# Running sums of a linear attention from pairs of tokens, in whole 32-bit products

## The reference, cut to what matters

```python
x = L0_attn_x
xn = _layernorm(x, axis=-1)
x = x + _L0_attn_ref(xn, ...) + _L0_ffn_ref(xn, ...)     # experts: top 2 of 8
# in _L0_attn_ref, per batch and head, with q, k after rope and elu + 1:
def step(carry, qkv):
    K_sum, KV = carry
    q_t, k_t, v_t = qkv
    K_sum = K_sum + k_t
    KV = KV + k_t[..., :, None] * v_t[..., None, :]
    num = jnp.einsum('bhd,bhde->bhe', q_t, KV)
    den = jnp.maximum(jnp.einsum('bhd,bhd->bh', q_t, K_sum), EPS)
    return ((K_sum, KV), num / den[..., None])
xn = _layernorm(x, axis=-1)
x = x + _L1_attn_ref(xn, ...) + _L1_ffn_ref(xn, ...)     # ffn reads x_prev, the token before
```

## Time and profile before

| what | value |
|---|---|
| median of three runs | 368.72 us |
| the profiled execution's own time | 367.48 us |
| its span, first to last instruction | 365.7 us |
| PE busy, of the span | 347.7 us (95%) |
| DVE busy | 317.6 us (87%) |
| ACT busy | 276.1 us (75%) |
| POOL busy | 204.3 us (56%) |
| granted TensorE clock, mean | 0.999 of full speed |

### The profile page before, as it was taken

The page is one execution under the profiler, slowest core; times in us unless marked ns, Lnnn a source line. Parts: engine busy times, 40 slices in busy tenths (PEclk is TensorE's granted clock), DMA queues, the critical chain, the costliest instruction groups (busy, mean ns, idle before and its releaser), DMA issues.

```text
span 365.7 us, 9318 instructions
## 1 busy us (share of the span) xinstructions
PE 347.7 (95%) x2534; PEld 299.9 (82%) x2534; DVE 317.6 (87%) x623; ACT 276.1 (75%) x774; POOL 204.3 (56%) x239
## 2 busy tenths in 40 slices
PE   7999988799899999999999899999999899999986
PEld 2788534499799999999999799989989688788875
DVE  3998799559989999999699979998996799998665
ACT  3887967777686877787878767787895987778752
POOL 3899118844234465756665648675857448883110
PEclk9999999999999999999999999999999999999999
DMA  6842848555355555655654554756642102221112
GB/s 182 217 124 74 325 192 234 173 149 134 108 133 137 139 143 146 170 139 150 175 143 135 152 161 129 186 150 152 148 115 70 31 2 57 57 61 29 30 29 59
DMA packets 45521, 47.00 MB, mean 129 GB/s; under 512 B 6928, under 2 KB 33712, under 8 KB 45216
## 3 DMA queue, kind: packets, MB, share of 16 engines
q1 hardware_dynamic: 40288, 36.88, 33.6%
q0 software_dynamic: 4320, 8.86, 11.5%
q10 hardware_dynamic: 864, 0.67, 0.7%
HBM read 32.88 MB, written 13.50 MB: 127 GB/s over the span
## 4 chain that ended last, share of the span: by engine, by line
PE 76%; DVE 14%; issue 3%; ACT 3%; DMA 2%; ACTq 1%; DVEq 0%
PE banks L546 16%; PE banks L534 14%; PE banks L674 6%; PE banks L675 6%; PE banks L330 3%; PE banks L983 3%; PE banks L1010 2%; PE banks L299 2%; PE banks L524 2%; PE banks L1039 2%; PE banks L321 2%; PE banks L1019 2%; PE banks L993 2%; PE banks L1057 2%; DVE cq L686 2%
## 5 line engine op out<-in xcount | busy, mean ns | idle before, releaser
L468 POOL DMA_INDIRECT xg<-xn_rows,slot_tok x71 | 74.8, 1053 | 74.2 <-PE banks L524 61.7
L563 ACT ACTIVATE xT<-banks,b1T 128x128 f32<-128x128 f32 x284 | 81.1, 371 | 15.4 <-PE banks L534 14.7
L546 PE MATMUL banks<-w_sb,xT 128*128 x568 | 79.6, 283 | 0.0
L485 POOL DMA_INDIRECT qk_exp<-expert_rows,ranki x64 | 63.7, 996 | 21.6 <-issue 17.9
L534 PE MATMUL banks<-xgT,w 128*128 128x128 f32 x568 | 75.3, 276 | 0.0
L546 PEld LDWEIGHTS banks<-w_sb,xT 128*128 128x128 f32 x568 | 69.3, 192 | 1.2
L534 PEld LDWEIGHTS banks<-xgT,w 128*128 128x128 f32 x568 | 69.0, 192 | 0.0
L686 DVE TENSOR_TENSOR cq<-banks,phi 128x360 f32<-128x360 f32 (+1 forms) x96 | 47.4, 548 | 19.1 <-PE banks L675 18.9
L652 ACT CAST high<-outer 128x1152 fp32r<-128x1152 f32 x32 | 37.1, 1158 | 21.6 <-DVE outer L641 21.2
L658 DVE TENSOR_TENSOR low<-outer,high 128x1152 fp32r<-128x1152 f32 x32 | 43.3, 1352 | 3.2 <-ACT high L652 3.2
L695 DVE TENSOR_REDUCE sums<-cq 128x144 f32<-128x1152 f32 x32 | 42.9, 1341 | 0.0
(11 more groups left out here) (205 smaller groups left out, 702.7 us busy)
## 6 DMA issues: line engine op xcount, KB each, us to landing
w<-in_L_ffn_W SPq DMA_DIRECT2D x71, 256.0 KB
expert_rows<-ye SPq DMA_DIRECT2D x71, 64.0 KB
expert_rows<-x_sb SPq DMA_DIRECT2D x2, 2048.0 KB, 10.6
x_sb<-in_L_attn_x SPq DMA_DIRECT2D x8, 256.0 KB, 4.3
xn_rows<-xn SPq DMA_DIRECT2D x8, 256.0 KB, 2.3
w_sb<-in_L_ffn_W SPq DMA_DIRECT2D x8, 256.0 KB, 4.5
out<-outer SPq DMA_DIRECT2D x7, 256.0 KB, 2.3
xg<-xn_rows,slot_tok POOLq DMA_INDIRECT x71
```

The source lines that it names most:

```text
L468: pool.indirect_dma_start(out=xg[n][:, :], out_offset=None, in_=xn_dram, in_offset=bass.IndirectOffsetOnAxis(ap=slot_tok[:, j:j + 1], axis ...
L485: pool.indirect_dma_start(out=y_moe[:, i, k, :], out_offset=None, in_=y_dram, in_offset=bass.IndirectOffsetOnAxis(ap=ranki[:, 0, k, i:i + ...
L546: last = nc.tensor.matmul(y, hidT[p][:, c, :], w2_sb[:, ds(e * NC + c, 1), :], start=False, stop=(c == NC - 1))
L563: last = nc.scalar.activation(hidT[p][:, c, :], ps[3 + p][:, c * P:(c + 1) * P], ACT.Gelu_apprx_tanh, bias=b1T[:, ds(e * NC + c, 1)])
```

## The change

A batch's two tiles now hold its even tokens (r = 0) and its odd tokens (r = 1), so row p of both is the pair of tokens 2p and 2p + 1. DVE adds the outer products of the two (`attn_pair`, 128 x 1152, once per batch). PE multiplies this sum, as plain 32-bit data, with the triangle that leaves the own row out (`tri_x`) for the even tokens, and with the one that includes it (`tri_r`) for the odd ones. An even token then lacks its own term; POOL computes it as (q . k) v in five small instructions per batch (`attn_own`), and DVE adds it to the sums (`attn_add_own`). `high`, `low` and their casts and subtractions are gone. DVE now makes phi and both outer products of the next batch in the even tile, and the pair in the odd tile. ACT copies both tiles' keys in one place.

The loads and stores of x, of the normalised x and of the output are written so that the two tiles of a batch are one run of 1 KB per partition. In the second layer, blocks of 128 columns are swapped (`block_of`), and `mix` takes four instructions of half the size.

```diff
+    pair = [sbuf(f"pair{n}", [P, HED])[:, :] for n in range(2)]
+    tri_r = sbuf("tri_r", [P, P])
+    tri_x = sbuf("tri_x", [P, P])
...
-    def attn_high(act, b, r, p):
-        i = b * 2 + r
-        act.wait_ge(outer_ready, i + 1)
-        act.wait_ge(den_ready, i + 1)
-        if from_(b, 2 - r):
-            act.wait_ge(cum_ps, b * 2 - (0 if r else 2))
-        nc.scalar.copy(high[kept(r, p)], outer[r]).then_inc(high_ready, 1)
-    def attn_low(v, b, r, p):
-        v.wait_ge(high_ready, b * 2 + r + 1)
-        n = kept(r, p)
-        nc.vector.tensor_tensor(low[n], outer[r], high[n].bitcast(f32), ALU.subtract).then_inc(low_ready, 1)
+    def attn_pair(v, b, p):
+        v.wait_ge(outer_ready, 2 * b + 2)
+        v.wait_ge(den_ready, 2 * b + 2)
+        if b >= 2:
+            v.wait_ge(cum_ps, 2 * b - 2)
+        nc.vector.tensor_tensor(pair[p], outer[0], outer[1], ALU.add).then_inc(pair_ready, 1)
+    def attn_own(pool, b, p):
+        pool.wait_ge(phi_ready, b + 1)
+        if b >= 2:
+            pool.wait_ge(own_used, b - 1)
+        nc.gpsimd.tensor_tensor(own_qk[:, :], phib[p][:, 0, 0:D], phib[p][:, 0, D:2 * D], ALU.mult).then_inc(own_part, 1)
+        q = own_qk[:, :].rearrange("p (h d) -> p h d", d=DH)
+        n = 4 * b + 1
+        for half in (DH // 2, DH // 4):
+            pool.wait_ge(own_part, n)
+            nc.gpsimd.tensor_tensor(q[:, :, 0:half], q[:, :, 0:half], q[:, :, half:2 * half], ALU.add).then_inc(own_part, 1)
+            n += 1
+        pool.wait_ge(own_part, n)
+        nc.gpsimd.tensor_tensor(own_dot[:, :], q[:, :, 0], q[:, :, 1], ALU.add).then_inc(own_part, 1)
...
+        nc.gpsimd.tensor_tensor(own[p][:, :, :], own_dot[:, :].unsqueeze(2).broadcast_to([P, H, E9]),
+                                qkv3[:, 2 * b, 2 * D:NW].rearrange("p (e h) -> p h e", h=H), ALU.mult).then_inc(own_ready, 1)
+    def attn_add_own(v, b, p):
+        v.wait_ge(own_ready, b + 1)
+        v.wait_ge(sums_ready, 2 * b + 1)
+        nc.vector.tensor_tensor(sums[:, 0, :, :], sums[:, 0, :, :], own[p][:, :, :], ALU.add).then_inc(own_used, 1)
...
-        pe.wait_ge(low_ready, i + 1)
-        parts = [(tri_r, kept(r, p))] + ([(ones_r, kept(0, p))] if r else [])
+        pe.wait_ge(pair_ready, b + 1)
+        w = tri_r if r else tri_x
         for n, (lo, hi) in enumerate(HEADS):
             cols = slice(lo * E9 * DH, hi * E9 * DH)
             o = ps[n][:, 0:(hi - lo) * E9 * DH]
-            for m, (w, at) in enumerate(parts):
-                nc.tensor.matmul(o, w[:, :], high[at][:, cols], start=(m == 0), stop=False)
-                last = nc.tensor.matmul(o, w[:, :], low[at][:, cols], start=False, stop=(m == len(parts) - 1))
+            last = nc.tensor.matmul(o, w[:, :], pair[p][:, cols], start=True, stop=True)
...
+    OWN_AT = [max(SUMS_AT[2 * b] - 3, 0) for b in range(B)]
...
+            for lo, to in ((P + 1, 0), (0, P)):
+                t = mix_t[p][m].rearrange("p (b t) -> p b t", t=T)[:, :, to:to + P]
+                last = nc.vector.scalar_tensor_tensor(out=t, in0=xT2_of(p)[:, :, lo:lo + P], scalar=one_mu[:, m:m + 1],
+                                                      in1=t, op0=ALU.mult, op1=ALU.add)
...
             def odd(i):
-                if i + 2 < NT:
-                    attn_keys(act, i // 2 + 1, i % 2, 1 - i // 2 % 2)
-                    attn_high(act, i // 2 + 1, i % 2, 1 - i // 2 % 2)
+                if i % 2 == 0 and i + 2 < NT:
+                    for r in range(2):
+                        attn_keys(act, i // 2 + 1, r, 1 - i // 2 % 2)
...
             pool.wait_ge(logits_read, len(CHUNKS))
+            nc.gpsimd.memset(qkv3[:, :, 3 * D:NW], 1.0).then_inc(ones_ready, 1)
...
+                if j in OWN_AT:
+                    attn_own(pool, OWN_AT.index(j), OWN_AT.index(j) % 2)
...
+                if r == 0:
+                    if b + 1 < B:
+                        phi(v, b + 1, 1 - p)
+                        for t in range(2):
+                            attn_outer(v, b + 1, t, 1 - p)
+                    attn_sums(v, i, r)
+                else:
+                    if b + 1 < B:
+                        attn_pair(v, b + 1, 1 - p)
+                    attn_add_own(v, b, p)
+                    attn_sums(v, i, r)
```

More of the change, by code:

```diff
@@ L60, in constant_table @@
     put("rows_in_front", P * row)
-    put("token_no", P * np.arange(NT)[None, :] + row - TOK // 2)
+    n = np.arange(NT)[None, :]
+    put("token_no", n // 2 * T + 2 * row + n % 2 - TOK // 2)
     return c
@@ L170, in build @@
     outer = [sbuf(f"outer{n}", [P, HED])[:, :] for n in range(2)]
-    high = [sbuf(f"high{n}", [P, HED], f32r)[:, :] for n in range(3)]
-    low = [sbuf(f"low{n}", [P, HED], f32r)[:, :] for n in range(3)]
-    def kept(r, p):
-        return 2 if r else p
+    pair = [sbuf(f"pair{n}", [P, HED])[:, :] for n in range(2)]
     w_raw = outer[0][:, 0:8 * P].rearrange("p (n c) -> p n c", c=P)
-    tri_r = sbuf("tri_r", [P, P], f32r)
-    ones_r = sbuf("ones_r", [P, P], f32r)
+    tri_r = sbuf("tri_r", [P, P])
+    tri_x = sbuf("tri_x", [P, P])
+    ones_r = sbuf("ones_r", [P, P])
+    own_qk, own_dot = sbuf("own_qk", [P, D]), sbuf("own_dot", [P, H])
+    own = [sbuf("own", [P, H, E9]), by_turn[:, :, :].rearrange("p a s -> p (a s)").rearrange("p (h e) -> p h e", e=E9)]
     cq = sbuf("cq", [P, HED])[:, :]
@@ L761, in build, with steps @@
     Y_STEP = [SUMS_AT[2 * b + 2] + 1 for b in range(B)]
-    def steps(eng, expert_step, even, odd, first=None, second=None, last=None):
+    OWN_AT = [max(SUMS_AT[2 * b] - 3, 0) for b in range(B)]
+    def steps(eng, expert_step, even, odd, first=None, last=None):
         for j in range(-2, SUMS_AT[-1] + 2):
             between, behind = None, False
-            if j == SUMS_AT[0] - 2:
-                between = second
-            elif j in SUMS_AT:
+            if j in SUMS_AT:
                 between = functools.partial(even, SUMS_AT.index(j))
@@ L851, in xT2_transpose @@
         for n in range(GT):
-            last = nc.tensor.transpose(ps[1][:, n * P:(n + 1) * P], xn[g % NB][:, n, :], ident)
+            last = nc.tensor.transpose(ps[1][:, block_of(n)], xn[g % NB][:, n, :], ident)
         last.then_inc(xT2_ps, 1)
@@ L1388, in _ @@
             nc.scalar.activation(scrap["scalar"], scrap["zero"], ACT.Gelu_apprx_tanh).then_inc(warmed, 1)
-            def first():
-                for r in range(2):
-                    attn_keys(act, 0, r, 0)
-                attn_high(act, 0, 0, 0)
-            def second():
-                attn_high(act, 0, 1, 0)
+            for r in range(2):
+                attn_keys(act, 0, r, 0)
             steps(act, lambda act, base, s, between=None, batch=None, behind=False, first=None: expert_scalar(
@@ L1399, in _ @@
                   even, odd,
-                  first=first, second=second, last=last)
+                  last=last)
             groups(act, group_scalar)
@@ L1687, in tile @@
                 attn_apply(v, b, r, p)
[L1690 to L1695 removed]
+                if r == 0:
[9 more added lines that the diff above has]
+                    attn_sums(v, i, r)
                     attn_reciprocal(v, b)
                     attn_divide(v, b)
[L1698 to L1701 removed]
+            phi(v, 0, 0)
             for r in range(2):
                 attn_outer(v, 0, r, 0)
[L1704 removed]
+            attn_pair(v, 0, 0)
             for b in range(B):
```

86 lines of the change are left out of this document (39 added, 47 removed).

## The result

The changed kernel takes 373.98 us (median of four runs, 372.66 to 374.35), the kernel before 368.52 beside it: a ratio of 1.0137 (95% interval 1.0100 to 1.0174), 5.5 us slower. Executions on these chips fall into a faster and a slower state and every ratio here is taken from the faster ones alone, so it can differ from that of the two medians. The prediction was 376.7 us, with a range from 371.5 to 382.5 and 0.89 for slower.

A forecast was written before the change was run, and what follows sets the result against it. PE was taken to pace the second stage, DVE close behind. Products +10.4, waits -4, stage's end +0.4, mixes +0.4 and POOL/DVE interference +0.8 gave +8.0 on the 368.7 us median: 376.7 us, range 371.5 to 382.5.

The forecast's parts named there:

- Products, +10.4: Second stage, PE's running sums: plain 32-bit products instead of halves cost 0.65 us more per batch, +10.4 us in all.
- Four passes: PE's running sums: true FP32 takes four passes through the array; by exactly four the loss would be 17 us.
- rival (c): PE's running sums: each 32-bit record runs at the half's rate, so whole products are cheap: 348 us, chance 0.04.
- Waits that PE gets back, -4: Second stage: PE's waits on the removed casts and subtractions go, -3.2 us, and smaller ones, -0.8: -4 us.
- Rival (b): Second stage: every wait of PE goes, about 10 us in all, giving 370 us; chance 0.13.
- DVE, 0 by itself: Second stage: DVE saves about 1 us per batch, worth nothing by itself since PE paces.
- Rival (d): Second stage: the even tile's work is late on DVE, 5 us more, 381 us; chance 0.08.
- POOL, 0 to +5 and +0.8 taken: Second stage: POOL's own term charged 0, possibly up to +5 us; +0.8 for POOL and DVE hindering each other.
- Rival (a): Second stage: POOL becomes the bound if the own term exceeds 5 us per batch: +5 more, 381.7 us; chance 0.13.
- The stage's end and the mixes, +0.4 and +0.4: Second stage's end: short addition and first mix, +0.2 each; seven further mixes beside PE, +0.4 us (0 to 1.5).
- First stage, 0: First stage: one more ACT copy, 0.26 us, and fewer, longer loads of x: 0, from -0.3 to +0.3 us.
- my 219 to 222: Sign that the forecast was right: the second stage takes 219 to 222 us.

The follow-up runs named there:

- experiment 4: Changed kernel with POOL computing the own term for the first two batches only, later batches taking a stale one: 372.00 us, ratio 1.0076 to the kernel before.
- experiment 3: Changed kernel with two casts per batch put back on ACT, into buffers nobody reads: 379.62 us, ratio 1.0305 to the kernel before.
- 6 and 10: Kernel before with its cast into the high half one step later on ACT, run on two other chips: ratios 1.0222 and 1.0057 to the kernel before.
- experiment 1: The one-pass kernel: changed kernel with the pair rounded for one PE pass, its low half left out: 368.48 us, ratio 0.9969 to the kernel before.
- experiment 7: Changed kernel with the mix as one 128x512 instruction instead of two of 128x256, on another chip: 401.19 us, ratio 1.0236 to the kernel before.

## Why the prediction was right

- *Products, +10.4*: measured +11.3. The new side was right to the hundredth (1.94 us per tile, 3.88 per batch against 3.89). The half products of before hold PE for 50.75/16 = 3.17 us per batch, where I had 3.22 to 3.34 from single places (3.33 is the sum over the stage without the correction for the early first record); the sum over the stage was to be had before.
- *Four passes*: the 32-bit record at 0.303 us stands against 0.168 for a half product; the whole product costs 3.6 halves, as the rows gave, and rival (c), a cheap whole product, is out.
- *Waits that PE gets back, -4*: this term was mis-sized. They gave -7.8, and with experiment 4's 2 us, which POOL takes mostly from the same gaps, nearly 10. I had priced the three stalls that the profile names (3.2 us), and no more than 0.8 for the small ones: many gaps of under 0.4 us, none of which stands out in a list of waits. Ahead of the bias product, for one, 14 of the 38 gaps behind up products were longer than their usual 0.11 us before, and 2 are now. Rival (b) named this amount, "about 10 in all", with 0.13. That the casts on ACT made most of them is supported by experiment 3 (put back, they cost 5.5 us of the stage); their place alone was not tested on the first chip, and moving it (6 and 10) gained nothing on the others.
- *DVE, 0 by itself*: right, no DVE line is left in the chain. Rival (d), an even tile late on DVE, did not come, although its outer products grew by 0.13 us each.
- *POOL, 0 to +5 and +0.8 taken*: the own term takes 2.97 us on average, within 2.1 to 4.2, and costs 2 us. Two of its five instructions stand beside the outer products, as I expected, but the second and third, and in eight batches of sixteen. Rival (a), POOL as the bound, didn't come in this kernel, but its distance was smaller than I thought: take the products away and PE waits 20.1 us for gathers (experiment 1).
- *First transposes*: the clock at its 1.2 GHz level for 3.4 us, +1.1 us within the up products, was in no term. It stands in this trace and not in the one before by chance: most runs of both kernels have such a stretch. The 1.2 us by which the median of before lies above its profiled run fit it.
- *The stage's end and the mixes, +0.4 and +0.4*: the third stage grew by 1.5. I had thought seven mixes mostly hidden beside PE; experiment 7 shows that 0.15 us of each group's period comes from them.
- *First stage, 0*: +0.2.

With the sizes as measured: 11.3 - 7.8 + 1.1 + 1.5 + 0.2 = +6.3, the difference of the spans. My sum of +8.0 was 1.7 too high on the profiled execution (375.5 against 373.86); the other 1.1 us of the miss are the 1.2 that I added for the median of before, which the changed kernel's median (373.98) doesn't have. The waits' error (3.8) was hidden in part by costs that were too low: products 0.9, clock 1.1, third stage 0.7, first 0.2. That the total came so close is in this part luck. So is the stage's 219.65 us within my 219 to 222, which I had counted from a stage of 213.5 us and not from the 215.0 that it took.

## What to carry to other kernels

Count a 32-bit matrix product at 3.6 times a half one before trading halves for fewer products: three for six is a loss, three for twelve only a small gain. When an instruction leaves an engine that others wait for in order, price what it held up, by the sum of all gaps between the pacing engine's records, not by the few waits that a list names. And when one engine's load falls, look at the next in line first: here products cheaper by 41 us brought 5.5, and the chain of waits then ran through GpSimd's gathers and own terms. Last, look at the two values behind a mean, and at the clock of all runs, before a difference between two traces is called the change's.

## What the runs showed of the hardware

- VectorE and GpSimd slow each other. An outer product of 128x1024 takes 1.340 us with own terms on GpSimd, 1.239 with two of them left, 1.213 in the kernel before, which has none. A 128x64 addition on GpSimd takes 1.18 to 1.20 us beside an outer product, until that has ended, and 0.32 otherwise, eight times each and never anything between.
- TensorE's granted clock dropped to 0.5 for 3.4 us after idle time of PE: in the changed kernel at 69.7 us, behind a wait of 1.65 us for `xg`, in the one-pass kernel at about 70 too, at 176 behind a wait of 2.58 us, and for 6.8 us from 230.6 on, within a wait of 4.58 us. The trace of the kernel before has a wait of 1.48 us at the first place and no drop, but by their mean clock 17 of 22 other runs of it had one somewhere. One such stretch cost the changed kernel 1.2 to 1.7 us.
- The same kernel was 1.4% slower than the other on one chip and 5.5% on another, where the kernel before took 382.65 us instead of 368.5; the changed kernel's running sums took the same time on both, the waits between the products did not. In the eight traces from the slower chips, and in no other, engines pause together for an event that no instruction in the profile accounts for.
